# Query product of the latent attention by high and low f16 parts, with the first tile's keys and half of its query product inside the fold

## The reference

```python
q_hk  = (hidden_q @ Wq.T).reshape(b, s, H, K)               # H = 16, K = 128
q_big = einsum('bshk,hkq->bshq', q_hk, w_kc_q)              # 192
kv_rope = kv_c * cos[None] + _rotate_half(kv_c) * sin[None] # 257 x 64
q_r = einsum('bshq,hqr->bhsr', q_big, W_qr)
k_r = einsum('bld,hdr->bhlr', kv_rope, W_kr)
attn = softmax(einsum('bhsr,bhlr->bhsl', q_r, k_r))
ctx_c = einsum('bhsl,bld->bhsd', attn, kv_rope)             # 64 a head
out = einsum('bhsd,hkd->bshk', ctx_c, w_kc_kv).reshape(b, s, H * K) @ Wo.T
# then x = x + out, self attention (w = codes * scales), experts (top 8 of 64)
```

## Time and profile before

| | |
|---|---|
| profiled execution | 742.43 us, span 740.4 us |
| runs | 743.28 us (742.62 to 745.24) |
| busy, share of the span: TensorE matmuls | 86% |
| TensorE weight loads | 74% |
| VectorE | 61% |
| ScalarE | 39% |
| GpSimd | 35% |
| mean granted clock of TensorE | 0.929 |

### The profile page before, as it was taken

The page is one execution under the profiler, slowest core; times in us unless marked ns, Lnnn a source line. Parts: engine busy times, 40 slices in busy tenths (PEclk is TensorE's granted clock), DMA queues, the critical chain, the costliest instruction groups (busy, mean ns, idle before and its releaser), DMA issues.

```text
span 740.4 us, 16762 instructions
## 1 busy us (share of the span) xinstructions
PE 634.2 (86%) x6373; PEld 546.4 (74%) x6373; DVE 453.3 (61%) x1246; ACT 285.9 (39%) x788; POOL 258.7 (35%) x281
## 2 busy tenths in 40 slices
PE   5998576699999998999999999999888879999910
PEld 4887555598788797788798788797777767778900
DVE  1135475556577686777677677677575335555648
ACT  1112365334635634634635635635412033333400
POOL 3202568521121441341441441410404325555620
PEclk9996656699999999999999999999999999999965
DMA  7974799299030230140140110100101759999567
GB/s 197 274 197 112 177 244 226 59 298 296 24 113 3 68 132 2 38 162 3 41 159 2 47 39 2 41 25 2 61 2 47 219 149 330 330 322 305 150 253 298
DMA packets 93503, 100.83 MB, mean 136 GB/s; under 512 B 26560, under 2 KB 84473, under 8 KB 92401
## 3 DMA queue, kind: packets, MB, share of 16 engines
q1 hardware_dynamic: 86672, 83.38, 39.1%
q0 software_dynamic: 6144, 15.96, 5.9%
q10 hardware_dynamic: 608, 0.42, 0.2%
HBM read 65.17 MB, written 36.18 MB: 137 GB/s over the span
## 4 chain that ended last, share of the span: by engine, by line
PE 57%; DVE 18%; DMA 8%; ACT 8%; issue 6%; SPq 2%; POOL 2%; POOLq 0%; DVEq 0%; PEldq 0%; ACTq 0%
PE bank L1452 6%; PE bank L1226 6%; PE bank L1228 6%; PE bank L1227 5%; PE bank L1259 4%; PE bank L1291 4%; DMA Wh<-expert_rows 4%; PE bank L1340 3%; PE bank L1245 3%; PE bank L1461 2%; PE bank L1280 2%; PE bank L1215 2%; PE bank L1443 2%; PE bank L1203 2%; ACT diag L693 2%
## 5 line engine op out<-in xcount | busy, mean ns | idle before, releaser
L655 ACT ACTIVATE pr<-bank,nmax 128x257 f32<-128x257 f32 x128 | 61.3, 479 | 96.1 <-DVE nmax L873 95.7
L1226 PE MATMUL bank<-space,Wh 128*128 128x128 f16 x512 | 88.1, 219 | 0.3
L1228 PE MATMUL bank<-space,Wl 128*128 128x128 f16 x512 | 88.1, 219 | 0.0
L1227 PE MATMUL bank<-space,Wh 128*128 128x128 f16 x512 | 88.1, 219 | 0.0
L533 POOL DMA_INDIRECT expert_rows<-h,slot x64 | 62.9, 983 | 64.7 <-DVE slot L970 48.9
L516 POOL TENSOR_TENSOR Cr<-C,Ct 128x192 f32<-128x192 f32 x64 | 40.7, 658 | 121.1 <-PE bank L1291 110.9
L595 POOL DMA_INDIRECT pair_rows<-Wh,etok x64 | 62.2, 972 | 54.0 <-issue 30.2
L873 DVE TENSOR_REDUCE nmax<-bank 128x1 f32<-128x257 f32 x128 | 53.3, 421 | 43.4 <-PE bank L1273 41.2
L1291 PE MATMUL bank<-Cr,pT 128*128 128x64 f32 x512 | 75.6, 273 | 0.1
L1291 PEld LDWEIGHTS bank<-Cr,pT 128*128 128x128 f32 x512 | 72.2, 204 | 0.2 <-ACT pT L663 0.2
L663 ACT COPY pT<-bank 128x256 f32<-128x256 f32 x128 | 47.5, 371 | 63.1 <-PE bank L1280 61.0
(11 more groups left out here) (191 smaller groups left out, 1526.2 us busy)
## 6 DMA issues: line engine op xcount, KB each, us to landing
expert_rows<-h SPq DMA_DIRECT2D x8, 1120.0 KB, 13.7
Wh<-expert_rows SPq DMA_DIRECT2D x64, 140.0 KB, 3.9
pair_rows<-zrow SPq DMA_DIRECT2D x8, 1024.0 KB, 9.1
Wl<-L_ffn_gate_up_proj_dram SPq DMA_DIRECT2D x36, 192.0 KB, 3.8
ring<-L_ffn_gate_up_proj_dram SPq DMA_DIRECT2D x28, 192.0 KB, 3.7
space<-pair_rows SPq DMA_DIRECT2D x5, 1024.0 KB, 8.9
Wl<-L_ffn_down_proj_dram SPq DMA_DIRECT2D x36, 96.0 KB, 4.7
C<-ctx_dram SPq DMA_DIRECT2D x24, 128.0 KB, 3.8
```

The lines of the kernel that those rows point to most:

```text
L655: e.activation(pr[:, s, :], bank[r % 2][:, 0:NL], ACT.Exp, bias=nmax[:, s:s + 1], accum_out=rsum[:, s:s + 1]).then_inc(expd, 1)
L1226: e.matmul(dst, ah, bh, start=first and n == 0, stop=False)
L1227: e.matmul(dst, ah, bl, start=False, stop=False)
L1228: ins = e.matmul(dst, al, bh, start=False, stop=last and n == len(terms) - 1)
```

## The change

`M` is kept as two f16 matrices in the same memory: `Mh`, `M` times 256 rounded, and `Ml`, the rest. `h1T` likewise becomes `h1Th` and `h1Tl`. A query product is three f16 matmuls (high by high, high by low, low by high), 24 a half in place of 8 in f32, and the copies of the result multiply by 1/256. The result's columns are laid out by sequence. ScalarE makes `h1Th`, VectorE `h1Tl` at step 13.

For the first tile `hT`, `kt0` and `qa` are issued inside the fold's last group, on TensorE between its G product and its Q product, in banks of their own; `qb` stays behind the fold. `fkqT` moves from the memory of the queries to a free piece of `space`. The norm of the first tile (`next_h1(0)`) is issued in the third group, and the parts that are left in a group are multiplied after the statistics and the norm, no longer before them.

```diff
-XSPLIT = ["kt1", "kt2", "kt3", "kt0", "qa", "qb"]
+XSPLIT = ["kt1", "kt2", "kt3", "hT", "kt0", "qa", "qb"]
-X_LOW_AT = {3: ["kt1"], 7: ["kt2"], 9: ["kt3"], 14: ["kt0"], 15: ["qa"], 16: ["qb"]}
+X_LOW_AT = {3: ["kt1"], 7: ["kt2"], 9: ["kt3"], 13: ["hT"], 14: ["kt0"], 15: ["qa"], 16: ["qb"]}
+MS = 256.0
+        Mh, Ml = (M[:, n, :].bitcast(f16).rearrange("p (c n) -> p c n", c=DCH) for n in range(2))
+        h1Th, h1Tl = (h1T[:, n, :].bitcast(f16).rearrange("p (c t) -> p c t", c=DCH) for n in range(2))
-        fkqT = qspace[0:QC, :].rearrange("p (h c d) -> p h c d", h=GH, c=2)
+        fkqT = cut(GH * 2 * P, QC).rearrange("p (h c d) -> p h c d", h=GH, c=2)
+        X0_BANK = {"hT": 2, "kt0": 3, "qa": 4, "qb": 6}
-            dst = q2[parity][DC * half:DC * half + DC, :, a:a + 4, :].rearrange("p b c s -> p c b s")
+            dst = q2[parity][DC * half:DC * half + DC, :, a:a + 4, :].rearrange("p b c s -> p b (c s)")
...
         # ScalarE
                 if name == "hT":
-                    dst, s = h1T[:, :, :], src[:, 0:D].rearrange("p (c t) -> p c t", c=DCH)
+                    e.copy(h1Th, src[:, 0:D].rearrange("p (c t) -> p c t", c=DCH)).then_inc(x_high, 1)
+                    return
                 elif name in ("qa", "qb"):
                     for n in range(2):
                         dst, s = q_halves(name, n, n, src)
-                        ins = e.copy(dst, s)
+                        ins = e.mul(dst, s, 1.0 / MS)
...
+            for g in range(GROUPS):
+                e.wait_ge(f_b, g + 1)
...
+                if g == GROUPS - 1:
+                    e.sem_inc(x_high, XSPLIT.index("hT"))
+                    for name in XNEXT[:-1]:
+                        x_use(name, 0)
+                e.wait_ge(f_n, g + 1)
+                e.copy(N[:, 2 * g:2 * g + 2, :], ...).then_inc(f_na, 1)
+                for u in range(PART0[g], PART0[g + 1]):
+                    part_high(u)
+            x_use(XNEXT[-1], 0)
...
         # VectorE
+                elif name == "hT":
+                    ins = e.tensor_tensor(h1Tl, src[:, 0:D]..., h1Th, ALU.subtract)
-                        ins = e.tensor_tensor(q_halves(name, n, 1 - n, src)[0], s, high, ALU.subtract)
+                        ins = e.scalar_tensor_tensor(q_halves(name, n, 1 - n, src)[0], s, 1.0 / MS, high, ALU.mult, ALU.subtract)
...
+                if g == GROUPS - 1:
+                    for name in XNEXT[:-1]:
+                        x_low(name, 0)
+                if len(left) > 2:
+                    part_mul(left.pop(0))
...
-                e.tensor_copy(M[:, :, GH * DC * g:GH * DC * (g + 1)], ...).then_inc(f_md, 1)
-                for u in left:
-                    part_mul(u)
+                e.tensor_scalar(Mh[:, :, gs], bank[7]..., MS, None, ALU.mult).then_inc(f_mh, 1)
+                e.wait_ge(f_mh, g + 1)
+                e.scalar_tensor_tensor(Ml[:, :, gs], bank[7]..., MS, Mh[:, :, gs], ALU.mult, ALU.subtract).then_inc(f_md, 1)
                 if g in (1, 2):
                     all_stats(g - 1)
+                if g == 2:
+                    next_h1(0)
+                for u in left:
+                    part_mul(u)
+            x_low(XNEXT[-1], 0)
...
         # TensorE
-                        for k in range(DCH):
-                            ins = e.matmul(dst[:, n * P:(n + 1) * P], M[:, k, c * P:(c + 1) * P], h1T[:, k, :], start=k == 0, stop=k == DCH - 1)
+                        ins = split(dst.rearrange("p (b c s) -> p b c s", b=BT, c=4)[:, :, n, :],
+                                    [(Mh[:, k, c * P:(c + 1) * P], Ml[:, k, c * P:(c + 1) * P], h[:, k], lo[:, k]) for k in range(DCH)])
...
                 ins.then_inc(f_g, 1)
                 if g < GROUPS - 1:
                     rope_transposes(g + 1)
+                else:
+                    for name in XS[:XS.index("qb")]:
+                        (x_use(name, 0) if name in XNEXT else x_skip(name, -1))
                 e.wait_ge(f_gd, g + 1)
                 e.wait_ge(f_ta, g * 4 + 4)
...
             e.wait_ge(f_md, GROUPS)
             e.wait_ge(f_na, GROUPS)
-            for name in XS:
-                (x_use(name, 0) if name in XNEXT else x_skip(name, -1))
+            x_use("qb", 0)
             tile(0, None, None)
```

More of the change, by code:

```diff
@@ L284, in build, with xbank @@
         SBANK = (bank[6], bank[7])
+        X0_BANK = {"hT": 2, "kt0": 3, "qa": 4, "qb": 6}
+        def xbank(name, i):
+            if isinstance(i, int) and i == 0 and name in XNEXT:
+                return bank[X0_BANK[name]]
+            return XBANK[XS.index(name) % 2]
         def xpos(name, i, more=1):
@@ L610, in part_high @@
                 e.copy(part_of(Wh, u), parts[BUFFER[u]][:, 0]).then_inc(w_high, 1)
[L612 to L623, removed]
             def x_use(name, i):
                 bk_, need = xpos(name, i)
-                src = XBANK[bk_]
+                src = xbank(name, i)
                 e.wait_ge(xf[bk_], need)
                 if name == "hT":
-                    dst, s = h1T[:, :, :], src[:, 0:D].rearrange("p (c t) -> p c t", c=DCH)
+                    e.copy(h1Th, src[:, 0:D].rearrange("p (c t) -> p c t", c=DCH)).then_inc(x_high, 1)
+                    return
                 elif name in ("qa", "qb"):
@@ L1232, in x_use @@
                 bk_, need = xpos(name, i)
-                dst = XBANK[bk_]
-                e.wait_ge(xd[bk_], need - 1 + FREE)
+                dst = xbank(name, i)
+                if not (isinstance(i, int) and i == 0 and name == "qb"):
+                    e.wait_ge(xd[bk_], need - 1 + FREE)
                 if name == "hT":
@@ L1412, in tile @@
                             sum_row(i, r - 3)
+                        if isinstance(i, int) and i == 0 and r == 2:
+                            for name in XS[XS.index("qb") + 1:]:
+                                x_skip(name, -1)
                         for name in X_AT.get(r, ()):
@@ L1424, in tile @@
                         fill(FILL_AT[r])
-            for name in XS:
-                (x_use(name, 0) if name in XNEXT else x_skip(name, -1))
+            rope_transposes(0)
+            transposes(0)
+            for g in range(GROUPS):
+                e.wait_ge(f_td, g * 3 + 3)
+                if g:
+                    e.wait_ge(f_md, g)
+                for h in range(GH):
+                    for c in range(2):
+                        ins = e.matmul(bank[7][0:QC, (2 * h + c) * DC:(2 * h + c + 1) * DC], fqrT[:, h, c, :], fkrT[:, h, :], start=True, stop=True)
+                ins.then_inc(f_g, 1)
+                if g < GROUPS - 1:
+                    rope_transposes(g + 1)
+                else:
+                    for name in XS[:XS.index("qb")]:
+                        (x_use(name, 0) if name in XNEXT else x_skip(name, -1))
+                e.wait_ge(f_gd, g + 1)
+                e.wait_ge(f_ta, g * 4 + 4)
+                for h in range(GH):
+                    for c in range(2):
+                        ins = e.matmul(bank[0][:, h * DC:(h + 1) * DC], fkqT[:, h, c, :], fG[:, h, c, :], start=c == 0, stop=c == 1)
+                ins.then_inc(f_q, 1)
+                e.wait_ge(rest_in[g % 2], 32 * (g // 2) + 32)
+                for h in range(GH):
+                    q = DC * (h % 2)
+                    ins = e.matmul(bank[5][q:q + DC, (h // 2) * D:(h // 2 + 1) * D], fkv[g % 2][:, h, :], fWoT[:, h, :], start=True, stop=True)
+                ins.then_inc(f_n, 1)
+                e.wait_ge(f_qd, g + 1)
+                for h in range(GH):
+                    for c in range(DCH):
+                        ins = e.matmul(bank[7][:, c * 256 + h * DC:c * 256 + (h + 1) * DC], fWq[g % 2][:, h, c * P:(c + 1) * P], fQ[:, h, :], start=True, stop=True)
+                ins.then_inc(f_m, 1)
+                if g < GROUPS - 1:
+                    transposes(g + 1)
+            e.wait_ge(f_md, GROUPS)
+            e.wait_ge(f_na, GROUPS)
+            x_use("qb", 0)
             tile(0, None, None)
```

85 lines of the change are left out of this document (28 added, 57 removed).

## The result

The kernel after took 751.43 us in the median of 20 runs (742.58 to 759.66), the kernel before 744.18 beside it: a ratio of 1.0094, interval 1.0059 to 1.0129, some 7 us slower. The forecast was 745.8 with 749.0 as its upper end: the sign was right, the size was not.

What follows compares the result with a forecast made beforehand. Bounds: a DMA-bound first tile behind a fold, then tiles bound by TensorE with a ScalarE stretch. Sum 6.6 - 1.5 - 3.1 + 0.5 = +2.5 us, 744.9 for the profiled execution, 745.8 on the median's scale; range 740.0 to 749.0.

Steps and rivals of the forecast that it cites:

- The first halves in the tiles: Six tiles from 150 us: first query half 1.34 instead of 1.85 us, -3.1 us in all; second halves priced at nothing.
- the multiplying copies: ScalarE's copies of query halves, four a tile in seven tiles, now multiply: +0.5 us, bounds 0 and 0.8.
- Rival D: Weight loads bound the f16 matmuls, a half takes 2.38 us: +10.3 in all, 753.6 us; chance 0.05.
- rival E: VectorE's added low half of the transposed activations isn't hidden in the tiles: +5.4 in all, 748.7 us; chance 0.08.
- the sum over the tiles: Later tiles: -3.1 us from first query halves, copies +0.5 over seven tiles, the added VectorE low half taken as 0.
- The fold: Last fold group: query half ahead of the Q product delays part 5's issue from 78.36 to 84.9, +6.6 us, bounds 3.3 and 6.6.
- The idle TensorE: Sign in the fold's last group: TensorE idle from about 69 to 73 us.
- rival B: TensorE's clock is high in the fold's new order: shift 3.3, not 6.6; sum -0.8, 742.5 us; chance 0.20.
- part 13 lands as much later as part 5 is issued: First tile: the DMA stream from part 5 was never idle, so part 13 also lands 6.6 us later.
- 6.6 less 1.5: First tile: 6.6 us later from part 5's delay, less 1.5 from its two faster query halves.
- rival C: First tile bound by its own rows through buffer releases, not the stream's start: sum -3.4, 739.9 us; chance 0.17.
- no gain: Start of the first tile: first maximum at 92.8 us against 92.10 before, despite the moved query half.

Runs made afterwards that it cites:

- the kernel before with 64: Kernel before plus 64 TensorE instructions that only raise an unneeded semaphore, in steps 0 to 7 of the first tile: ratio 1.0129.
- the same kernel with 192 idle instructions: Kernel after plus 192 TensorE instructions that only raise an unneeded semaphore, in steps 0 to 11 of the first tile: ratio 1.0025.
- the half behind: Kernel after with parts multiplied ahead of statistics and first norm, and the first query half behind the fold; transposes and keys stay inside: ratio 0.9981.
- after, 165: Kernel after plus 165 idle TensorE instructions, 15 a step in steps 1 to 11 of the first tile: ratio 0.9993.
- 20 and 256: Kernel before plus 20 or 256 idle TensorE instructions in the first tile: ratios 1.0056 and 1.0037.
- 23 in the kernel after: Kernel after plus 23 idle TensorE instructions in steps 0 to 11 of the first tile: ratio 1.0105.
- The placement alone: Kernel before with transposes, first keys and first query half inside the fold's last group, parts multiplied behind statistics and norm, all f32: ratio 0.9981.
- the one of 256: Kernel after plus 256 idle TensorE instructions, 16 a step in the first tile: ratio 1.0180.
- Parts first: Kernel after with the parts left in a fold group multiplied before the statistics and the first norm: ratio 1.0084.
- the split alone: Kernel before with only the f16 split; the first tile's transposes, keys and both query halves stay behind the fold: ratio 1.0060.

## Why the prediction was wrong

**The first halves in the tiles: right.** Forecast 6 x 0.51 less 0.5 for the multiplying copies, -2.6. A half took 1.34 us, as forecast. In B, split kernels with one stop of 1.5 to 2.0 stand at 379.0 in the mean, f32 kernels with one of 2.1 to 2.7 at 383.4: -4.4. About 0.7 of it is the difference of the stops and up to 1.7 the low clock of 3.4 us that stands behind the f32 kernels' stop and not behind one of 1.7 us; that leaves -2.0 to -3.7, around the forecast. A closer pair has a large stop on both sides: the kernel before with 64 (4.67) has B 386.3, the three split kernels with one (4.77 to 5.35) 383.8 in the mean, -2.5. Rival D (weight loads) and rival E (VectorE) are out: either would have made B longer.

**The step that failed: the sum over the tiles had no term for instruction fetch.** It took the tiles of after as the tiles of before less 0.51. In B the kernel after lies 8.4 us above the same kernel with 192 idle instructions (387.3 against 378.9, stops of 7.04 against 1.70 us; the remaining 3 us go with the low clock behind them). So B is -5.4 + 8.4 = +3.0. By the ratios it is 6.3 us: 1.0094 against 1.0025 and 0.9993, mean 1.0009. The interval of 0.9993 (to 1.0035) lies wholly below that of 1.0094 (from 1.0059); that of 1.0025 reaches into it. The kernels with the half behind show it in B (383.8 to 378.6), but hardly in the ratio (0.9981, then 0.9946 with 192 and 0.9985 with 165). That the ends of the blocks make the stops is shown, by moving them to and fro; that the wait is for the fetch is shown by the packets, each of which ended 1.24 to 1.64 us before TensorE went on.

**The fold: right in its chain, too large in what it passes on.** Counted from the third `M` copy:

| | forecast | after | after, 165 |
|---|---|---|---|
| part 1 multiplied | 4.3 | 4.1 | 4.1 |
| query half begins | 9.5 | 9.2 | 9.2 |
| last `M` copy | 21.1 | 18.4 | 20.9 |
| part 5 issued (before 14.7) | 21.2 | 19.4 | 21.0 |

The idle TensorE was there (4.14 us), then the query half in 2.5 at the low clock. In the profiled run of after the clock then rose to 0.98, as in rival B, and the shift was 4.7, between its 3.3 and my 6.6. With 165 the clock stayed at 0.50 and the chain came out as I had forecast it, to 0.3 us:

```profile
63.00:74.00 11.00, 10.58 (x56) 9.14 (x53) 4.55 (x6) 3.66 (x5) 2.38 (x2) 0.50 0.30 83
```

The fold that is left as it was varies too: in the kernel before and its versions with 64, 20 and 256 part 5 is issued at 14.7, 17.3, 15.4 and 15.4, so that the shift of 4.7 goes by the earliest of them. Over all four (mean 15.7) and the five kernels with the fold of after (20.5) it is 4.8.

What failed is the prediction's next sentence, that part 13 lands as much later as part 5 is issued. Of 4.7 us at part 5 there were 1.1 left at part 11 (38.3 against 37.2 behind the `M` copy), then 2.7 at the issue of part 13 (45.2 against 42.5), 3.5 at its multiplication (63.2 against 59.7) and 2.8 at the first output product. Forecast for that point was 6.6 less 1.5, +5.1. So rival C's mechanism holds in part: the later parts follow the tile's own rows, and the first row came 1.8 us earlier (26.6 against 28.4) where I had forecast no gain. It isn't of one trace: with 20 idle instructions in the kernel before the row comes at 30.1, with 23 in the kernel after at 28.2. The placement alone shows it best: part 5 7.2 us later, A 1.4 shorter. Why the delay grew again from part 11 to 13 is not settled.

**The fold's share.** A is 83.4 us in the mean of five kernels with the f16 half ahead of the Q product (without the one of 256) and 80.5 in the four with it behind the fold. The ratios of the pairs that differ only in this and in the order of the parts: 1.0025 to 0.9946, 1.0105 to 0.9984, 0.9993 to 0.9985, so 0.8, 1.2 and 0.1 per cent, each uncertain by over half a per cent. Parts first against half behind is the purest pair (1.0084 to 0.9981, 1.0 per cent), but the first has one stop of 2.49 us more. Some 3 to 5 us; the pair with 165 fits nothing as well, and the size stays open. A scatters too: the split alone, all behind the fold, has 81.0 and with 192 idle instructions 86.1. Part order: after against parts first, 1.0094 and 1.0084, no difference.

**The sum with the measured terms:** fold and first tile +2.8, tiles -5.4, stops and their clock +8.4: +5.8 of the 7.0 (4.4 to 9.6). The +2.8 rests on two single traces; the other two terms are borne out by several kernels each. The forecast had +5.1 and -2.6 for the first two and nothing for the third: the fold's error hid part of what the missing term cost. No version was shown to beat the kernel before: the half behind the fold has 0.9946 with 192 idle instructions and 0.9985 with 165, both with an interval that holds 1.

## What to carry to other kernels

When a change alters how many instructions an engine runs, the ends of its instruction blocks move for the rest of the program; a stretch that runs through a whole block in 1 to 2 us near such an end (here 64 tiny f32 matmuls) can then stop TensorE for 2 to 5 us, and that may be larger than the change. Look in the trace of before for gaps "issue" on TensorE, count the records modulo 256, set the 16 KB instruction packets beside them, and work out where the ends will fall; and before a small loss is put down to an edit, move the ends with empty instructions, and test their own cost with a whole block of them. A delay at the head of a chain of buffer releases need not arrive at its end: take it at each release, not once.

## What the hardware showed unexpectedly

- TensorE stopped for 1.5 to 5.4 us before records 193 to 195 modulo 256, 23 times in 17 traces (the kernel before, the kernel after and 15 others, each with one or two). The block's end falls into the densest stretch (256 records in 1.3 us) or within some 50 records behind it.
- No block of 256 began sooner than 1.23 us behind the end of its 16 KB instruction packet (886 block starts), and packet n served block n + 1, as if TensorE held two.
- The stop was 4.5 to 5.4 us while the DMA engines moved 300 to 340 GB/s, 2.2 at 287, and 1.5 to 2.7 us while they were idle. The packet took about 1.1 us under that load too; it started later.
- With the stops of 1.96 us and more the granted clock fell to 0.5 for 3.4 to 6.8 us; behind those of 1.51 to 1.70 it stayed at 1.0.
- 64 instructions without work made the kernel before slower by 1.29% (0.75 to 1.83), in part by a stop that they moved into tile 1. In a row they start 0.15 us apart.
